# A grouped 3x7 convolution on TensorE: from tiles of 64x64 alone to dense 64x64 tiles plus 32x32 tiles for the single taps

## The chip, the cores and the metric

The kernel runs on one core of a Trainium2 chip (trn2). The metric is the device time of one execution in microseconds (us), the median of the runs. All data and all arithmetic are float32. TensorE is called PE here, its weight loads PEld, VectorE DVE, ScalarE ACT, GpSimd POOL and the engine that issues the DMAs SP, as the profile does.

## The reference

For each of 8 images x of 128 channels and 64x64 pixels:

```
t1  = p1_w * x                        # p1_w: one value for each channel and row
t2  = x + t1
t7  = p7_w @ relu(x)                  # 128x128 over the channels
t12 = mean over the 21 taps of (x - shifted t7)     # five distinct shifts in w
t11 = t1 (128 x 4096) times unfold3x7(x)^T          # 128 x (128*21)
t10 = grouped product of t2 with p10_w              # (128*21) x 4096
out = maximum(t11 @ t10 * scale, t12)
```

The kernel does not build t10 and t11. It first contracts p10_w with the unfolded x for each group of 32 channels, which is a convolution of 3 rows by 7 columns with 32 channels in and 32 out, in 4 groups (y). Then A = y times t1 transposed, a 128x128 matrix for each image, and the output's first operand is A times t2.

## The kernel before, in words

**Units and planes.** There are 32 units (u), one for each image n and group g = u % 4. The three taps in the row direction are done by a minimal-filtering scheme: pairs of image rows and four linear combinations (planes V_0, V_2, V_1, V_3 of `v_planes`, made by DVE from the loaded `xw`), with four planes of weights (`u_planes`, three loaded, then combined by three additions in `weights`). Products with planes 1 and 2 give the sum and difference from which `seeds` makes the starting values of the two banks of the unit, and products with planes 0 and 3 are accumulated on top.

**The seven column taps.** The 64 columns are 16 blocks of 4 phases. The 128 partitions of a plane are 4 phases by 32 channels. A matmul takes 64 partitions (two phases) and gives 64 outputs (a pair of phases by 32 channels) from one block shift, over 512 columns (16 blocks by 32 row pairs). `tiles` does two such matmuls for one shift i and one half of the partitions; together two calls fill the four 64x64 tiles of the array. A unit has four products of planes 1 and 2 (`one_two`, first or second, i of 0 and 1) and four of planes 0 and 3 (`zero_three`). Each of these eight calls issues four matmuls, one in each quarter of the array. The weight tiles hold zeros where a tap falls outside of the seven. In this text such a set of four 64x64 matmuls of 512 columns is called a step. Each float32 matmul shows in the profile as two MATMUL and two LDWEIGHTS records.

**A slot.** The program of PE is written out by hand. In the steady part, `slot(u, ...)` issues the eight convolution steps of planes 1 and 2 of unit u and of planes 0 and 3 of unit u-1, and between them two output items, each with two steps (`outputs_first`, `outputs_second`). An item is one half (512 pixels by 128 channels) of the product p7 with the box sums of relu(x), and another half of the product A times t2. That makes 12 steps. One slot in four has also `y_times_t1`, 32 products of 128 columns, and it is called the y slot here. Slots 0 to 5 and the part after unit 31 are written out apart.

**Dependences inside a slot.** `pq_half`, `m_half` and `item_half` are semaphores by which PE waits for its own earlier matmuls, since the second half of the rows adds to the same place in PSUM. When planes 1 and 2 of u are done (`pq_done`), ACT copies one bank (`copy_two`), DVE computes two seeds (`seeds`), and PE may start planes 0 and 3 of u in the next slot. When those are done (`m_done`), DVE transposes y (`turn_y`), and a new unit may use the banks (three sets) and the planes (three buffers).

**Other work.** DVE also makes the planes of a coming unit (`planes_low`, `planes_high`), the box sums (three operations on 1,024 pixels: `box_pairs`, `box_fours`, `box_last`) and the final maximum (`max_half`, L538). ACT does relu, t2 as eight small activations (`t2_half`, L314), the start values of the p7 banks (`seed_x`) and the copy of p7's result (`base_half`). POOL computes t1 (L219) and the weights of groups 2 and 3. All DMAs are issued by SP in one fixed order, with `load_group` for `xw`. Every order of work is written by hand; there is no planner.

## Time and profile before

| | before |
|---|---|
| median of 3 runs | 413.93 us (413.47 to 414.99) |
| the profiled execution | 411.89 us |
| its span in the profile | 409.9 us |
| PE busy | 398.8 us (97%) |
| DVE busy | 333.6 us (81%) |
| ACT busy | 249.4 us (61%) |
| POOL busy | 90.0 us (22%) |
| DMA | 72.40 MB, mean 177 GB/s |

The span is what the profile shows between the first and the last instruction; the profiled execution took about 2 us more than its span, and the median of the runs is another 2 us above it. A busy PE in this table is PE with at least one matmul running, not PE at its peak, since four tiles of the array can work at once.

### The profile page before, as it was taken

What the parts mean: (1) busy time and instruction counts of PE and PEld (TensorE: products, weight loads), DVE (VectorE), ACT (ScalarE), POOL (GpSimd) and SP (SyncE); (2) the same over time, 40 slices, a digit from 0 to 9 for tenths busy, and PEclk for the clock granted to TensorE, in tenths of its full rate; (3) what the DMA queues carried; (4) which work ended last, traced back from release to release, by engine and by line L of the source; (5) the groups of instructions that cost most, each with busy time, mean ns of one, the idle gap of its engine ahead of it and who ended that gap; (6) DMA issues with size and microseconds to landing.
All of it is one profiled execution on the core that took longest, in us unless ns stands there. A gap on an engine that the chain in (4) does not pass through costs nothing.

```text
span 409.9 us, 12373 instructions
## 1 busy us (share of the span) xinstructions
PE 398.8 (97%) x5126; PEld 250.5 (61%) x5126; DVE 333.6 (81%) x401; ACT 249.4 (61%) x714; POOL 90.0 (22%) x75
## 2 busy tenths in 40 slices
PE   7999999999999999999999999999999999999995
PEld 2333655668655586666888886444766668443663
DVE  6999968899788887888888887888868888786904
ACT  1336728777377755777277771777727775477970
POOL 0582200232023300332003320033202330033300
PEclk9999999999999999999999999999999999999999
DMA  8973263644665447663475635645455542632105
GB/s 295 406 304 109 86 238 116 210 162 158 206 197 176 151 140 221 191 224 104 169 241 201 203 117 187 232 164 164 163 209 187 169 157 80 216 128 95 54 28 206
DMA packets 24104, 72.40 MB, mean 177 GB/s; under 512 B 2800, under 2 KB 3056, under 8 KB 24048
## 3 DMA queue, kind: packets, MB, share of 16 engines
q1 hardware_dynamic: 24048, 71.61, 51.4%
q8 instruction: 41, 0.67, 0.7%
q14 instruction: 15, 0.12, 0.1%
HBM read 54.82 MB, written 16.78 MB: 175 GB/s over the span
## 4 chain that ended last, share of the span: by engine, by line
PE 84%; issue 6%; POOL 3%; DVE 3%; ACT 2%; DMA 2%; DVEq 0%; SPq 0%; ACTq 0%; POOLq 0%
PE ps_y L654 44%; PE ps_y L666 16%; PE ps_p L666 12%; PE ps_t L666 12%; POOL t1T L219 3%; DMA xw<-x_conv 2%; ACT t L314 1%; DVE v_planes L463 0%; DVE v_planes L440 0%; DVE yT L495 0%; DVE v_planes L449 0%; ACT base L259 0%; DVE base L538 0%; ACT relu_pad L272 0%; DVEq L43 0%
## 5 line engine op out<-in xcount | busy, mean ns | idle before, releaser
L654 PE MATMUL ps_y<-v_planes,u_planes 64*64 64x512 f32 x2048 | 257.0, 590 | 0.4
L654 PEld LDWEIGHTS ps_y<-v_planes,u_planes 64*64 64x64 f32 x2048 | 126.1, 133 | 93.6 <-issue 54.7
L219 POOL TENSOR_TENSOR t1T<-t1T,p1T_sb 128x512 f32<-128x512 f32 x64 | 84.1, 1340 | 281.4 <-DVE box L513 152.2
L314 ACT ACTIVATE t<-xn,p_plus 128x64 f32<-128x64 f32 x512 | 128.1, 335 | 0.0
L666 PE MATMUL ps_p<-box,p_fifth 64*64 64x512 f32 x464 | 123.4, 590 | 1.6 <-ACT ps_p L259 1.0
L666 PE MATMUL ps_t<-t,aT 64*64 64x512 f32 x448 | 118.4, 590 | 0.0
L259 ACT ACTIVATE base<-ps_p 128x512 f32<-128x512 f32 x58 | 34.6, 596 | 85.4 <-PE ps_p L666 85.4
L666 PEld LDWEIGHTS ps_y<-t1T,yT 64*64 64x64 f32 x2048 | 58.0, 133 | 8.4 <-DVE yT L495 5.0
L666 PE MATMUL ps_y<-t1T,yT 64*64 64x128 f32 x2048 | 60.7, 270 | 2.0 <-issue 1.2
L666 PEld LDWEIGHTS ps_p<-box,p_fifth 64*64 64x64 f32 x464 | 38.3, 133 | 22.7 <-issue 13.8
L482 DVE SCALAR_TENSOR_TENSOR ps_y<-ps_y,q_sb 128x512 f32<-128x512 f32 x32 | 22.3, 698 | 33.8 <-ACT q_sb L259 33.7
L538 DVE TENSOR_TENSOR base<-ps_t,base 128x512 f32<-128x512 f32 x56 | 38.4, 686 | 12.3 <-PE ps_t L666 11.8
L666 PEld LDWEIGHTS ps_t<-t,aT 64*64 64x64 f32 x448 | 37.2, 133 | 18.0 <-issue 4.9
L505 DVE TENSOR_TENSOR pair_sum<-relu_pad 128x1120 f32<-128x1120 f32 x32 | 42.5, 1328 | 0.0
L495 DVE STREAM_TRANSPOSE yT<-ps_y 128x512 f32<-128x512 f32 x64 | 41.7, 690 | 0.0
L463 DVE TENSOR_TENSOR v_planes<-xw 128x1152 f32<-128x1152 f32 x30 | 41.4, 1381 | 0.0
L522 DVE TENSOR_TENSOR box<-box,relu_pad 128x1024 f32<-128x1024 f32 x32 | 39.1, 1223 | 0.9
L513 DVE TENSOR_TENSOR box<-pair_sum 128x1024 f32<-128x1024 f32 x32 | 39.1, 1223 | 0.8
L259 ACT ACTIVATE ps_p<-xn 128x512 f32<-128x512 f32 x58 | 34.9, 602 | 6.7 <-ACT base L259 0.4
L272 ACT ACTIVATE relu_pad<-xn 128x1024 f32<-128x1024 f32 x32 | 33.7, 1053 | 1.8 <-DVE box L522 1.8
L259 ACT ACTIVATE q_sb<-ps_y 128x512 f32<-128x512 f32 x32 | 18.6, 583 | 24.7 <-PE ps_y L654 24.7
L471 DVE TENSOR_TENSOR v_planes<-xw 128x576 f32<-128x576 f32 x30 | 24.0, 801 | 0.0
(42 smaller groups left out, 119.2 us busy)
## 6 DMA issues: line engine op xcount, KB each, us to landing
xw<-x_conv SPq DMA_DIRECT2D x32, 594.0 KB, 5.4
xn<-x_nat SPq DMA_DIRECT2D x32, 512.0 KB, 4.1
t1T<-x_pix SPq DMA_DIRECT2D x32, 512.0 KB, 6.1
out<-base SPq DMA_DIRECT2D x64, 256.0 KB, 2.5
u_planes<-w_tiles SPq DMA_DIRECT2D x4, 384.0 KB, 7.1
p1T_sb<-p1T SPq DMA_DIRECT2D x1, 128.0 KB, 7.5
p_sb<-p7T SPq DMA_DIRECT2D x1, 64.0 KB, 7.3
p_sb<-p SPq DMA_DIRECT2D x1, 32.0 KB, 7.8
```

What stands on the lines that cost most here:

```text
L219: nc.gpsimd.tensor_tensor(part, part, p1T_sb[:, e, :].unsqueeze(1).broadcast_to([P, 4, C]), ALU.mult).then_inc(t1_ready, 1)
L259: return nc.scalar.activation(dst, src, ACT.Copy, scale=scale)
L272: nc.scalar.activation(relu_pad[:, i % 2, :, LO:LO + W], xn[:, f, :].rearrange("p (a b) -> p a b", b=W), ACT.Relu).then_inc(relu_ready, 1)
L314: last = nc.scalar.activation(t2[:, h, W * r:W * (r + 1)], xn[:, f, at:at + W], ACT.Copy, scale=p1_plus[:, 8 * h + r:8 * h + r + 1])
L463: nc.vector.tensor_tensor(v_planes[:, b, V_0:V_2 + 1], xw[:, b, :, :, 0:PAIRS], second, ALU.subtract).then_inc(v_ready, 1)
L495: nc.vector.transpose(yT[:, e, :, CG * g:CG * (g + 1)], ps_y[u % SETS][e][:].rearrange("p (j r) -> p j r", r=PAIRS)).then_inc(y_turned, 1)
L505: nc.vector.tensor_tensor(pair_sum[:], r[:, :, 0:PS_W], r[:, :, 3:3 + PS_W], ALU.add).then_inc(box_steps, 1)
L513: nc.vector.tensor_tensor(box[:, f, :].rearrange("p (a b) -> p a b", b=W), pair_sum[:, :, 0:W], pair_sum[:, :, 6:6 + W], ALU.add).then_inc ...
L522: nc.vector.tensor_tensor(dst, dst, relu_pad[:, i % 2, :, 12:12 + W], ALU.add).then_inc(box_steps, 1)
L538: nc.vector.tensor_tensor(base[:, h, :], t13_bank(n, h)[:], base[:, h, :], ALU.max).then_inc(out_ready, 1)
L654: last = nc.tensor.matmul(dst[TILE * pair:TILE * pair + TILE, :], u_planes[rows, u % GROUPS, weights, TILE * k:TILE * k + TILE], v_planes[ ...
L666: last = nc.tensor.matmul(dst[cols, 0:data.shape[-1]], weights[rows, cols], data[rows, :], start=start, stop=False, skip_group_check=True)
```

## The change

The seven taps of an output phase are split in another way. For an output pair of phases there are three products of 64 partitions by 64 outputs whose weight tile is full (dense), and what is left are single taps: one 32x32 product for each of the four input phases in each plane. So a plane needs three steps' share of 64x64 tiles and four 32x32 tiles. The three dense calls replace four, and the single taps of four planes (planes 1 and 2 of u, planes 0 and 3 of u-1) are put at the end of the slot as sixteen 32x32 matmuls of 512 columns in sixteen different places of the array (`single_taps`). A semaphore `dense_done` makes PE wait for the dense matmuls before them.

So that the sixteen tiles fall on sixteen places, the phases of x lie on the partitions in different orders: FRONT for planes 0 and 2, BACK for planes 1 and 3, and both differ by the parity of the unit (`PHASES_OF`). x is therefore loaded twice for each unit, with 19 blocks where there were 18: twice 642,048 bytes where there were 608,256. The weights of a group come in both orders: 688,128 bytes where there were 393,216.

`pq_done` of u and `m_done` of u-1 now both come at the end of slot u. In consequence the orders of ACT and DVE are changed: at the start of a slot ACT has `copy_two`, and DVE has `turn_y` and then `seeds`; relu and t2 and the box sums move. In the beginning, the weights are loaded ahead of the x of their group and slots 0 to 3 are written as slots; at the end `turn_y` of the last unit stands before a box sum, and the orders around the last A are changed.

```
-U_0, U_2, U_3, U_1 = range(4)
+FRONT, BACK = range(2)
+U_0, U_2, U_1, U_3 = (FRONT, 0), (FRONT, 1), (BACK, 1), (BACK, 2)
+PHASES_OF = {(0, FRONT): (1, 2, 3, 4), (0, BACK): (3, 4, 1, 2), (1, FRONT): (2, 1, 4, 3), (1, BACK): (4, 3, 2, 1)}
+DENSE = {True: ((0, 1), (0, 2), (1, 2)), False: ((1, 1), (1, 2), (0, 1))}
+SINGLE = {4: (0, 0), 3: (1, 2), 2: (2, 1), 1: (3, 3)}
...
-                sp.dma_start(xw[:, u % 3], x_conv[u // GROUPS, u % GROUPS]).then_inc(xw_loaded[u % 3], 16)
+                for order in range(2):
+                    sp.dma_start(xw[:, u % 3, order], x_conv[u // GROUPS, u % GROUPS, order]).then_inc(
+                        xw_loaded[u % 3][order], 16)
...
+            def dense(u, k, planes, start=False):
+                for half in range(2):
+                    for dst, weights, data in planes:
+                        pair, at = DENSE[low_phases(ORDER_OF[data], half)][k]
+                        last = nc.tensor.matmul(
+                            dst[TILE * pair:TILE * pair + TILE, :], weights_of(rows_of(half), u, weights, TILE * k, TILE),
+                            data_of(rows_of(half), u, data, at), start=start, stop=False, skip_group_check=True)
+                return last
+            def singles(u, planes):
+                for dst, weights, data in planes:
+                    for quarter, phase in enumerate(PHASES_OF[u % 2, ORDER_OF[data]]):
+                        rows = slice(SMALL_TILE * quarter, SMALL_TILE * quarter + SMALL_TILE)
+                        to, at = SINGLE[phase]
+                        last = nc.tensor.matmul(
+                            dst[SMALL_TILE * to:SMALL_TILE * to + SMALL_TILE, :],
+                            weights_of(rows, u, weights, 3 * TILE, SMALL_TILE),
+                            data_of(rows, u, data, at), start=False, stop=False, skip_group_check=True)
+                return last
+            def single_taps(u):
+                pe.wait_ge(dense_done, u + 1)
+                if u < UNITS:
+                    singles(u, planes_12(u)).then_inc(pq_done, 1)
+                if u > 0:
+                    singles(u - 1, planes_03(u - 1)).then_inc(m_done, 1)
...
             def slot(u, p_a, t_a, p_b, t_b, turned=None):
+                one_two(u, 0)
                 outputs_first(p_a, t_a, item_a)
-                one_two(u, True, 0)
+                one_two(u, 1)
                 outputs_second(p_a, t_a, item_a)
                 if turned is not None:
                     y_times_t1(turned)
-                one_two(u, True, 1)
-                zero_three(u - 1, True, 0)
-                zero_three(u - 1, True, 1)
+                one_two(u, 2)
+                zero_three(u - 1, 0)
+                zero_three(u - 1, 1)
                 outputs_first(p_b, t_b, item_b)
-                one_two(u, False, 0)
+                zero_three(u - 1, 2)
                 outputs_second(p_b, t_b, item_b)
-                one_two(u, False, 1)
-                zero_three(u - 1, False, 0)
-                zero_three(u - 1, False, 1)
+                single_taps(u)
```

## Rows read from the trace of the kernel before

**Rows 1.** The page: its first line, then part 1, busy time by engine.
```profile
span 409.9 us, 12373 instructions
...
PE 398.8 (97%) x5126; PEld 250.5 (61%) x5126; DVE 333.6 (81%) x401; ACT 249.4 (61%) x714; POOL 90.0 (22%) x75
```

**Rows 2.** The page, part 5: costliest groups, with busy time, mean ns and idle before.
```profile
L654 PE MATMUL ps_y<-v_planes,u_planes 64*64 64x512 f32 x2048 | 257.0, 590 | 0.4
...
L666 PE MATMUL ps_y<-t1T,yT 64*64 64x128 f32 x2048 | 60.7, 270 | 2.0 <-issue 1.2
```

**Rows 3.** Windows by stage: slots 0 to 3, slots 4 and 5, slots 6 to 31, the rest.
```profile
0.00:33.20 33.20, 30.70 (x234) 10.02 (x238) 29.79 (x36) 9.60 (x20) 13.94 (x15) 1.00 0.81 310
33.20:62.30 29.10, 28.27 (x446) 15.92 (x439) 24.17 (x28) 15.19 (x41) 5.02 (x4) 1.00 0.45 152
62.30:376.40 314.10, 311.79 (x4039) 207.45 (x4039) 262.69 (x316) 204.78 (x590) 67.44 (x54) 1.00 0.53 174
376.40:409.90 33.50, 28.00 (x428) 17.09 (x420) 16.94 (x23) 19.87 (x67) 3.59 (x2) 1.00 0.24 88
```

**Rows 4.** Windows of two plain slots and one y slot: PE, PEld, DVE, ACT, POOL.
```profile
269.50:279.80 10.30, 10.30 (x103) 4.97 (x99) 8.85 (x13) 7.72 (x23) 3.87 (x4) 1.00 0.58 188
...
290.10:308.20 18.10, 17.71 (x359) 13.52 (x355) 14.18 (x18) 8.02 (x24) 0.00 (x0) 1.00 0.56 196
```

**Rows 5.** PEld in order of time at the first steps: start, us, idle before.
```profile
8.52 0.14 PEld L654 LDWEIGHTS ps_y<-v_planes,u_planes 64*64 64x64 f32 x4 [0.29 <-issue]
9.65 0.21 PEld L654 LDWEIGHTS ps_y<-v_planes,u_planes 64*64 64x64 f32 x8 [0.98 <-PE ps_y L654]
10.13 0.15 PEld L654 LDWEIGHTS ps_y<-v_planes,u_planes 64*64 64x64 f32 x4 [0.28 <-issue]
```

**Rows 6.** PE in order of time where the tile size changes.
```profile
6.60 1.06 PE L811 MATMUL ps_p<-relu_pad 128*128 128x512 f32 x1
7.59 1.96 PE L654 MATMUL ps_y<-v_planes,u_planes 64*64 64x512 f32 x16
```

**Rows 7.** DVE in order of time, one plain slot.
```profile
281.01 1.32 DVE L463 TENSOR_TENSOR v_planes<-xw 128x1152 f32<-128x1152 f32 x1
282.25 0.68 DVE L538 TENSOR_TENSOR base<-ps_t,base 128x512 f32<-128x512 f32 x1
...
288.74 0.70 DVE L482 SCALAR_TENSOR_TENSOR ps_y<-ps_y,q_sb 128x512 f32<-128x512 f32 x1 [1.30 <-ACT q_sb L259]
289.48 0.70 DVE L485 SCALAR_TENSOR_TENSOR ps_y<-ps_y,q_sb 128x512 f32<-128x512 f32 x1
290.08 1.30 DVE L495 STREAM_TRANSPOSE yT<-ps_y 128x512 f32<-128x512 f32 x2
```

**Rows 8.** ACT in order of time, part of a slot.
```profile
276.51 0.60 ACT L259 ACTIVATE base<-ps_p 128x512 f32<-128x512 f32 x1 [1.90 <-PE ps_p L666]
277.22 0.60 ACT L259 ACTIVATE ps_p<-xn 128x512 f32<-128x512 f32 x1
277.76 0.58 ACT L259 ACTIVATE q_sb<-ps_y 128x512 f32<-128x512 f32 x1
278.23 2.01 ACT L314 ACTIVATE t<-xn,p_plus 128x64 f32<-128x64 f32 x8
```

**Rows 9.** Windows of the beginning; the last two columns are DMA share and GB/s.
```profile
2.50:5.00 2.50, 2.50 (x4) 0.95 (x4) 1.14 (x2) 0.00 (x0) 0.00 (x0) 1.00 1.01 358
...
20.00:25.00 5.00, 5.00 (x54) 1.70 (x47) 5.00 (x4) 0.63 (x2) 5.00 (x4) 1.00 1.02 409
```

**Rows 10.** DVE in order of time at the start: the first planes and weights.
```profile
4.75 0.76 DVE L436 TENSOR_TENSOR v_planes<-xw 128x576 f32<-128x576 f32 x1 [1.36 <-DMA xw<-x_conv]
...
7.00 0.42 DVE L429 TENSOR_TENSOR u_planes<-u_sum,u_planes 128x256 f32<-128x256 f32 x1
```

**Rows 11.** PE and ACT in order of time near the end.
```profile
386.35 3.72 PE L666 MATMUL ps_y<-t1T,yT 64*64 64x128 f32 x128 [0.41 <-DVE yT L495]
...
397.38 0.27 ACT L259 ACTIVATE a_part<-ps_y 128x128 f32<-128x128 f32 x1
```

More of the change, by code:

```diff
@@ L96, in conv_seq_kernel @@
         small_loaded = sem("small_loaded")
-        xw_loaded = [sem(f"xw_loaded{b}") for b in range(3)]
+        xw_loaded = [[sem(f"xw_loaded{b}{order}") for order in range(2)] for b in range(3)]
         xn_loaded = [sem(f"xn_loaded{f}") for f in range(4)]
@@ new lines, in _ @@
+            t2_half(1, 2)
+            base_half(1, 3)
+            seed_x(1, 4)
+            copy_two(8)
+            relu(2, 0)
+            t2_half(1, 3)
+            base_half(1, 4)
+            seed_x(1, 5)
+            first_part_of_a(1)
+            relu(2, 1)
+            t2_half(1, 4)
+            base_half(1, 5)
+            seed_x(1, 6)
+            t2_half(1, 5)
+            for n in range(2, N_IMG):
+                u = GROUPS * n
+                if n > 2:
+                    copy_two(u - 1)
@@ L566, in _ @@
             planes_high(4)
+            turn_y(2)
             seeds(3)
-            turn_y(2)
             box_sums(0, 1)
+            planes_low(5)
+            planes_high(5)
+            turn_y(3)
+            seeds(4)
+            box_sums(0, 2)
+            planes_low(6)
+            planes_high(6)
+            box_pairs(0, 3)
+            sum_of_a(0)
+            box_fours(0, 3)
+            box_last(0, 3)
+            box_pairs(1, 0)
+            max_half(0, 0)
             for n in range(1, N_IMG):
@@ new lines, in one_two, with zero_three @@
+                last = dense(u, k, planes_12(u), k == 0)
+                if k == 1:
+                    last.then_inc(pq_half, 1)
+                if k == 2 and u == 0:
+                    last.then_inc(dense_done, 1)
+            def zero_three(u, k):
+                if k == 0:
+                    pe.wait_ge(seeded, 2 * u + 2)
+                    pe.wait_ge(v_ready, 3 * u + 3)
+                if k == 2:
+                    pe.wait_ge(m_half, u + 1)
+                last = dense(u, k, planes_03(u))
+                if k == 1:
+                    last.then_inc(m_half, 1)
+                if k == 2:
+                    last.then_inc(dense_done, 1)
```

446 lines of the change are left out of this document (212 added, 234 removed).

## The prediction

> **What bounds the kernel now.** I began with the page's busy times [rows 1]. PE is busy 97% of the span, DVE 81%, ACT 61%. Then I read the costliest groups [rows 2], to see what PE does: 2,048 records of 64x64 by 512 columns for the convolution, 590 ns each, four at a time. The windows by stage [rows 3] split the span into a start of 33.2 us, two irregular slots of 29.1, slots 6 to 31 with 314.1, and an end of 33.5. In the third stage PE is busy 311.8 of 314.1 us. Single slots [rows 4, 7] show what one costs: the transposes of one slot begin 10.30 us before those of the next (289.48 is the seed just ahead of them), and a plain slot has twelve steps, so a step is 10.30 / 12 = 0.858 us, and a half step (one record in each of the four tiles) 0.429 us. All twelve run without a gap. The chain of PE's steps sets the time; DVE has 8.85 of 10.30 us of work in it and ends each slot with a wait of 1.30 us for ACT's copy of q. [...]
>
> **What is removed.** Each unit has six dense steps in place of eight. The sixteen 32x32 products, if they run together, stream 512 columns twice as every step does, so they are one step. A plain slot becomes 11 steps, 9.44 us. In slots 6 to 31, 26 slots, that is 26 x 0.858 = 22.3 us less.
>
> **What the small tiles add.** No record of before has 32x32 tiles, so the price is bounded. Below: nothing, if the array takes tiles of a new size behind running ones. Above, the nearest row is PE waiting for itself [rows 5]: the loads at 8.52 belong to the last half step ahead of a wait and those at 9.65 come after it. Half steps start 0.43 apart, the next would have begun at 8.52 + 2 x 0.43 = 9.38, and the one after the wait takes 10.13 - 9.65 = 0.48 instead of 0.43, as its weights were not loaded ahead. So a full stop with a semaphore costs 0.27 + 0.05 = 0.32 us. Without the semaphore's travel it is the record's tail, 0.590 - 0.429 = 0.16 [rows 2], plus 0.05: 0.21. There are two changes of size in a slot, into the small tiles and out. A load lasts some 0.13 us; four take 0.14 and eight 0.21 [rows 5], so starts follow each other by (0.14 - 0.13) / 3 to (0.21 - 0.13) / 7, 3 to 11 ns. I take 7: sixteen tiles start over 0.10 us. Range for a slot: 0 to 2 x 0.32 + 0.10 = 0.74 us. I take the stop without the semaphore twice, 0.42, plus 0.08 for the staggered start: 0.50 us. The one change of size in this trace [rows 6] speaks neither way: the 128x128 record starts at 6.60 and lasts 1.06, the 64x64 ones start at 7.59, and DVE gave their weights only at 7.00 + 0.42 [rows 10]; so there is at most 0.1 us between weights and matmul.
>
> [...]
>
> `dense_done` costs nothing of its own in a slot: `outputs_second`, one step of 0.858, lies between the last dense step and the wait, more than the 0.27 that a completion takes to come back. `pq_half`, `m_half` and `item_half` each have at least one step between, too. In slots 0 to 3 there is nothing between, and each costs 0.32.
>
> Sum for slots 6 to 31: -22.3 + 26 x 0.50 = -9.3.
>
> **DVE and ACT in a slot.** Both must fit in 9.94 us now. `planes_low` and `planes_high` grow by 1/18: 0.16 us on 1.32 + 0.75 + 0.75. So DVE has 9.0 us in a plain slot. In the y slot it has 14.2 + 0.2 + 1.3 (the `box_pairs` moved in) = 15.7 of about 17.4. It fits, and the wait for q of 1.30 is what paid for it. What has a deadline at the start of a slot: two transposes (1.30), two seeds (0.70 each, 0.73 apart [rows 7]), 0.3 for the completion; done at 3.1 us, and PE wants the seeds after five steps, at 4.3. Next `planes_low` and the first maximum end near 5.1, wanted at 7 steps, 6.0. ACT between slots: p7's copy and the next start value take 0.71 + 0.60 [rows 8]; with the completion (0.27) and the semaphore about 1.7 us, and PE leaves two steps plus the small tiles' extra, 1.7 + 0.5, where it left three steps. Only after the y slot is ACT late: `copy_two` stands behind the eight t2 activations (2.01 us [rows 8]) that stand behind the last start value. Counted from the next slot's start (c being the extra of a slot), start value 0.8 - c, t2 2.7 - c, q 3.3 - c, seeds 4.9 - c: with c = 0.50 that is 4.4 against 4.3, and the maximum behind them at 6.3 against 6.0. I add 0.3 us for six such slots: +1.8. Slots 6 to 31 then come to -7.5.
>
> **DMA.** x is 1.284 MB a unit where it was 0.608: 32 x 0.676 = 21.6 MB more, 72.4 to about 95 MB, with weights. In the steady part that is 174 GB/s [rows 3] plus 0.676 MB x 26 in 306 us, 57 GB/s: 231 of the 409 that the queue reached [rows 9]. It is hidden. POOL's products of t1 keep their gates.
>
> **The start.** There DMA is full from 2.5 to 25 us (share 1.01, 358 and then 409 GB/s [rows 9]). Bytes in order: w0 0.69 MB, x0 1.28, w1 0.69, x1 1.28, w2, x2, small ones, w3, x3. With the first window's 0.90 MB at 358 and then about 400 GB/s, and 1.0 us from the bytes to the landing (x0 of before: 0.61 MB at 3.8, used at 4.75 [rows 10]), x0 is whole at 8.7, its sum plane at 9.5, and PE starts at 9.7 where it started at 7.59 [rows 6]: +2.1. x1 lands at 13.7, just ahead of PE's need at 14.0 (+0.6 for its plane). Then 4 + 7 + 7 + 7 = 25 steps instead of 28, but with eleven uncovered waits at 0.32 (those ahead of the small tiles take the place of the first stop) where before had five, and four slots' second stop. By this account slot 3 ends at 36.2 where it ended at 33.2: +3.0 (between +1.5 and +5, as the DMA rate goes). Slots 4 and 5: two steps fewer (-1.7), +1.0 for small tiles, +0.4 as `early_first(2)` waits for box sums that come later in DVE's order: -0.3.
>
> **The end.** Planes 0 and 3 of unit 31 have three dense steps and half-filled small tiles, so no step is saved; +0.5. Seeds of unit 31 are ready 2.6 us after the slot's end (completion 0.27, q 0.58, seeds 0.73 + 0.70, three semaphores of 0.1) and PE has 2.0 of other work: +0.6 where it was 0.2, so +0.4. The transposes stand ahead of a box sum: y starts 0.56 earlier (of the 0.99 from the last output record to 386.35 [rows 11]). `first_part_of_a`, at 397.38 [rows 11], stays behind t2 and gains 0.2. Together +0.1.
>
> **Sum.** +3.0 - 0.3 - 7.5 + 0.1 = -4.7. The profiled execution's span 409.9 becomes 405.2, its own time 411.9 becomes 407.2. The median of the runs lies 2.0 above that execution, so 413.93 - 4.7 = 409.2, say 409. A change of 0.5% (2 us) is about what the measurement can tell; same means 411.9 to 416.0.
>
> **Rivals.**
> (a) Small tiles cost almost nothing (c about 0.1, the stagger alone). Then 31 x 0.4 = 12.4 us less, but more lateness of ACT after y slots, about 0.4 x 6 = 2.4: 399 us. For it: across different tiles PE already loads and starts independently, since in the y slot the LDWEIGHTS and MATMULs follow without gaps [rows 2]. Against: nothing shows it for another size.
> (b) The other side: the sixteen small products do not run sixteen at a time but eight. Then the stage is two steps, a slot is again 12 steps plus the extra: 31 x 0.858 = 26.6 us more, 436 us. For it: at most four tiles run together anywhere in this trace [rows 2], the float32 stream of four different inputs for each 32 partitions is twice what 64x64 tiles ask, and 64 records must be seen by PE at a time. It decides from a stage longer than 1.2 steps, since 4.7 / 32 = 0.15 us is all that each slot wins.
> [...]
> (c) The handover: both completions now come at the slot's end, and turns, seeds, planes and the first maximum form one chain with 0.9 to 1.2 us of slack, ACT's between slots with about 0.5. If 0.3 us more is lost in each of 26 slots: +8, 417 us. Against: DVE's slot [rows 7] with its present gaps fits.
>
> **How the numbers follow.** My forecast 0.45 (its own range 404 to 414: c from 0.35 to 0.65, start from +1.5 to +5); (a) 0.22; (b) 0.20; (c) 0.13. The range 395 to 425 leaves out (b) and the far end of (a). Faster by over 0.5%: 0.33 of my case, (a), 0.03 of (c): 0.58. Same: 0.09 + 0.04: 0.13. Slower: 0.29.
>
> **What would show it.** 32x32 records whose starts spread over 0.1 us and a gap of some 0.2 us on either side; plain slots 9.9 us apart; PE's first 64x64 at 9.7. A slot of 9.5 would show (a), one of 10.7 or more with small tiles in two or more waves (b), idle PE released by DVE seeds or ACT ps_p (c). My sum is wrong if the two stops are not 0.21 each, or if DMA in the start gets a different rate.

## The result

The changed kernel takes 411.22 us (median of 20 runs, 409.31 to 414.54); the kernel before, timed beside it, 413.46 us (20 runs, 412.13 to 415.10). The ratio is 0.9954, 95% interval 0.9932 to 0.9976: 2.2 us less, where 4.7 were forecast. That lies just within the 0.5% that the prediction called no change. The profiled execution is one of the shorter ones: 409.31 us, its span 407.5.

The page of the changed kernel, its first line, part 1, four of the costliest groups (busy us, mean ns, idle before) and the DMA line, beside [rows 1, 2]:

```profile
span 407.5 us, 13429 instructions
...
PE 386.6 (95%) x5638; PEld 181.5 (45%) x5638; DVE 341.9 (84%) x401; ACT 248.7 (61%) x714; POOL 88.4 (22%) x75
...
DMA packets 28717, 95.29 MB, mean 234 GB/s; under 512 B 3312, under 2 KB 3568, under 8 KB 28656
...
L731 PE MATMUL ps_y<-v_planes,u_planes 64*64 64x512 f32 x1536 | 197.2, 600 | 4.6 <-DVE v_planes L516 3.8
...
L753 PE MATMUL ps_y<-t1T,yT 64*64 64x128 f32 x2048 | 60.2, 270 | 5.4 <-issue 5.3
...
L742 PE MATMUL ps_y<-v_planes,u_planes 32*32 32x512 f32 x1024 | 38.2, 600 | 0.3
```

The dense records fell from 2,048 to 1,536 and 1,024 small ones came. PE is busy 12.2 us less, the span fell by only 2.4: PE is idle more. The products of `y_times_t1` waited 2.0 us in all before [rows 2] and wait 5.4 now. The stages, as in [rows 3] (slots 0 to 3; 4 and 5; 6 to 31; the rest):

```profile
0.00:36.50 36.50, 30.43 (x286) 8.17 (x286) 29.74 (x35) 8.31 (x17) 12.14 (x15) 0.95 0.97 384
36.50:65.80 29.30, 26.54 (x488) 14.36 (x472) 26.49 (x29) 18.03 (x49) 6.12 (x4) 1.00 0.72 267
65.80:374.30 308.50, 303.00 (x4464) 143.85 (x4448) 268.55 (x315) 203.14 (x587) 67.62 (x54) 1.00 0.67 228
374.30:407.50 33.20, 26.60 (x447) 15.11 (x432) 17.16 (x23) 19.26 (x63) 2.51 (x2) 1.00 0.26 97
```

| stage | forecast | measured |
|---|---|---|
| slots 0 to 3 | +3.0 | +3.3 |
| slots 4 and 5 | -0.3 | +0.2 |
| slots 6 to 31 | -7.5 | -5.6 |
| the rest | +0.1 | -0.3 |
| span | -4.7 | -2.4 |

The third stage holds most of the miss: 26 slots, 5.5 us without any PE work (308.50 - 303.00), where 2.3 were idle before [rows 3]. Its plain slots are near the forecast. Here PE around the small tiles, in order of time (start, us, records):

```profile
268.79 0.62 PE L753 MATMUL ps_p<-box,p_fifth 64*64 64x512 f32 x2
269.35 1.14 PE L742 MATMUL ps_y<-v_planes,u_planes 32*32 32x512 f32 x32
270.42 1.10 PE L731 MATMUL ps_y<-v_planes,u_planes 64*64 64x512 f32 x8
```

The 32 records of sixteen small products, which would be 32 x 0.6 us one after the other, take 1.14 us. The last half step ahead starts at 268.79 and leaves room for the next at 269.22 (0.43 later); the small tiles start at 269.35, and the next 64x64 at 270.42, which is 1.07 later where a step is 0.858. So the stage costs 0.13 + 1.07 = 1.20 us, 0.34 above a step; the small rest of the 0.42 by which a slot exceeds eleven steps lies outside of these rows. PE's weight loads in the same place take 0.23 us for all 32 records, in two passes of sixteen, so the sixteen tiles start over 0.1 us. PEld in order of time:

```profile
269.35 0.23 PEld L742 LDWEIGHTS ps_y<-v_planes,u_planes 32*32 32x32 f32 x32 [0.81 <-PE ps_y L731]
```

The transposes of DVE mark the slots. Those of two plain slots begin 9.84 us apart (146.48 - 136.64), forecast 9.94; the two around a y slot 18.05 (164.53 - 146.48):

```profile
136.64 1.31 DVE L555 STREAM_TRANSPOSE yT<-ps_y 128x512 f32<-128x512 f32 x2 [0.57 <-PE ps_y L742]
146.48 1.31 DVE L555 STREAM_TRANSPOSE yT<-ps_y 128x512 f32<-128x512 f32 x2 [0.56 <-PE ps_y L742]
164.53 1.31 DVE L555 STREAM_TRANSPOSE yT<-ps_y 128x512 f32<-128x512 f32 x2
```

Counted by PE's own last records a plain slot is 9.86 us, the slot behind each y slot 10.17 to 10.19 (+0.3, as forecast), and the six y slots are 20.93, 18.04, 17.37, 18.80, 17.37 and 16.92, together 109.4. Before, they were 17.34, 17.47, 18.24, 17.81, 18.10 and 17.66, together 106.6. The longest is the place to look. PE in order of time, the group behind the stall (in brackets the idle time before it), and under it windows of the same stretch (PE, PEld, DVE, ACT, POOL busy; granted clock, DMA share, GB/s):

```profile
109.12 0.97 PE L753 MATMUL ps_y<-t1T,yT 64*64 64x128 f32 x25 [2.73 <-issue]
```

```profile
101.00:106.90 5.90, 5.40 (x192) 5.15 (x184) 5.72 (x7) 0.60 (x1) 0.00 (x0) 1.00 0.94 331
106.90:109.10 2.20, 0.00 (x0) 0.00 (x0) 0.00 (x0) 0.00 (x0) 0.00 (x0) 1.00 0.11 36
```

From 101.0 to 106.9 the DMA engines are 94% busy: SP issued both orders of x for a coming unit at 100.04, the place where the old kernel issued one. When they are done, PE stands still for more than 2 us inside `y_times_t1`, with 26 of its 256 records to go (25 of them in the row above). No engine works, so none released it. "Issue" says only that the trace shows nothing that it waits for. The waits of that line in the changed kernel (total us, times, longest us); the old kernel's totals were 5.4 and 1.2 us:

```profile
PEld ps_y L753 <- issue: 14.3, 24, 3.0
...
PE ps_y L753 <- issue: 5.3, 4, 2.7
```

### The profile page after: what moved, and what is told of

Read it like the earlier page. It is cut to its first block, busy times and chain, and to the rows that moved or that the text cites. A ratio compares the mean times of both kernels' runs of the same rounds, so it can differ in the third digit from the quotient of the medians.

```text
span 407.5 us, 13429 instructions
## 1 busy us (share of the span) xinstructions
PE 386.6 (95%) x5638; PEld 181.5 (45%) x5638; DVE 341.9 (84%) x401; ACT 248.7 (61%) x714; POOL 88.4 (22%) x75
## 4 chain that ended last, share of the span: by engine, by line
PE 83%; DVE 9%; issue 4%; DMA 2%; ACT 1%; DVEq 0%; SPq 0%; ACTq 0%
PE ps_y L731 36%; PE ps_y L753 16%; PE ps_p L753 12%; PE ps_t L753 11%; PE ps_y L742 8%; DVE box L573 2%; DMA xw<-x_conv 2%; DVE pair_sum L565 2%; DVE yT L555 1%; DVE v_planes L510 1%; DVE v_planes L516 1%; DVE ps_y L542 1%; DVE base L598 1%; DVE v_planes L534 1%; DVE box L582 1%
## 5 line engine op out<-in xcount | busy, mean ns | idle before, releaser
L731 PE MATMUL ps_y<-v_planes,u_planes 64*64 64x512 f32 x1536 | 197.2, 600 | 4.6 <-DVE v_planes L516 3.8
L237 POOL TENSOR_TENSOR t1T<-t1T,p1T_sb 128x512 f32<-128x512 f32 x64 | 82.5, 1316 | 277.3 <-DVE box L582 238.7
L753 PE MATMUL ps_p<-box,p_fifth 64*64 64x512 f32 x464 | 120.1, 590 | 2.2 <-DVE box L582 1.7
L753 PE MATMUL ps_t<-t,aT 64*64 64x512 f32 x448 | 116.2, 591 | 0.1
L731 PEld LDWEIGHTS ps_y<-v_planes,u_planes 64*64 64x64 f32 x1536 | 63.5, 133 | 113.7 <-issue 88.1
L753 PEld LDWEIGHTS ps_y<-t1T,yT 64*64 64x64 f32 x2048 | 57.9, 133 | 11.7 <-issue 10.8
L510 DVE TENSOR_TENSOR v_planes<-xw 128x1216 f32<-128x1216 f32 x31 | 48.2, 1555 | 0.2 <-DMA xw<-x_conv 0.2
L753 PEld LDWEIGHTS ps_p<-box,p_fifth 64*64 64x64 f32 x464 | 34.0, 133 | 30.2 <-issue 21.1
L753 PEld LDWEIGHTS ps_t<-t,aT 64*64 64x64 f32 x448 | 32.5, 132 | 27.1 <-issue 12.5
L565 DVE TENSOR_TENSOR pair_sum<-relu_pad 128x1120 f32<-128x1120 f32 x32 | 43.2, 1350 | 0.0
L573 DVE TENSOR_TENSOR box<-pair_sum 128x1024 f32<-128x1024 f32 x32 | 41.1, 1283 | 0.6
L742 PE MATMUL ps_y<-v_planes,u_planes 32*32 32x512 f32 x1024 | 38.2, 600 | 0.3
L274 ACT ACTIVATE q_sb<-ps_y 128x512 f32<-128x512 f32 x32 | 18.6, 581 | 21.8 <-PE ps_y L742 21.8
## 6 DMA issues: line engine op xcount, KB each, us to landing
p1T_sb<-p1T SPq DMA_DIRECT2D x1, 128.0 KB, 12.2
p_sb<-p SPq DMA_DIRECT2D x1, 32.0 KB, 12.2
```

What stands on the lines that cost most here:

```text
L237: nc.gpsimd.tensor_tensor(part, part, p1T_sb[:, e, :].unsqueeze(1).broadcast_to([P, 4, C]), ALU.mult).then_inc(t1_ready, 1)
L274: return nc.scalar.activation(dst, src, ACT.Copy, scale=scale)
L510: nc.vector.tensor_tensor(v_planes[:, b, V_0:V_2 + 1], xw[:, b, FRONT, :, :, 0:PAIRS], second, ALU.subtract).then_inc(ready, 1)
L565: nc.vector.tensor_tensor(pair_sum[:], r[:, :, 0:PS_W], r[:, :, 3:3 + PS_W], ALU.add).then_inc(box_steps, 1)
L573: nc.vector.tensor_tensor(box[:, f, :].rearrange("p (a b) -> p a b", b=W), pair_sum[:, :, 0:W], pair_sum[:, :, 6:6 + W], ALU.add).then_inc ...
L731: last = nc.tensor.matmul(dst[TILE * pair:TILE * pair + TILE, :], weights_of(rows_of(half), u, weights, TILE * k, TILE), data_of(rows_of(h ...
```

## The experiments

Eleven kernels ran on the chip, each timed beside the kernel before. Medians and ratios are against it. The question was where the steady part's time stays, and then what the head and each size change cost.

| run | edit | median us (runs) | ratio (95%) |
|---|---|---|---|
| e1_warm | after + three zero matmuls at the start | 408.41 (6) | 0.9909 (0.9874 to 0.9943) |
| e2_same_size | after, four 64x64 for the sixteen 32x32 | 401.49 (4) | 0.9723 (0.9694 to 0.9751) |
| e3_one_order | after, second order of x not reloaded | 404.85 (6) | 0.9825 (0.9781 to 0.9868) |
| e4_quiet_y | after, one x load issued later | 402.76 (5) | 0.9746 (0.9717 to 0.9774) |
| e5_before_quiet_y | before, the same move | 409.78 (4) | 0.9913 (0.9898 to 0.9928) |
| e6_before_x_twice | before + x loaded again, unread | 425.88 (4) | 1.0298 (1.0281 to 1.0315) |
| e7_quiet_warm_head | e4 + e1 + orders of slot 4 | 401.06 (6) | 0.9699 (0.9685 to 0.9714) |
| e8_and_q_early | e7 + `copy_two` ahead of t2 | 399.60 (4) | 0.9668 (0.9653 to 0.9682) |
| e9_two_stages | after, small tiles in two stages | 436.61 (4) | 1.0581 (1.0544 to 1.0619) |
| e10_after_again | after, unchanged | 411.77 (12) | 0.9953 (0.9927 to 0.9979) |
| e11_split_y | after, `y_times_t1` in two halves | 411.52 (12) | 0.9971 (0.9952 to 0.999) |

### e1_warm: PE's clock in the head

In the changed kernel PE waits 2.77 us for the first planes, and its clock is granted at half (0.51 from 8.4 to 11.9 us) in the first steps. PE in order of time and the windows of that stretch:

```profile
8.77 4.66 PE L731 MATMUL ps_y<-v_planes,u_planes 64*64 64x512 f32 x24 [2.77 <-DVE v_planes L516]
```

```profile
8.40:11.90 3.50, 3.13 (x16) 0.80 (x16) 2.27 (x5) 0.00 (x0) 0.00 (x0) 0.51 1.00 415
```

```
+            for _ in range(3):
+                nc.tensor.matmul(ps_p7[:], zeros[:, 0:P], zeros[:, 0:HALF], start=True, stop=True)
             for bank_set in (ps_p7[:, 0:HALF // 2], ps_t13, ps_p7):
```

> The changed kernel with three more matmuls of zeros (128x128 by 512 columns) at PE's beginning, so that PE is busy until about 8.4 us instead of 5.9. In the profile of the changed kernel PE is idle from 6 to 8.8 us, its granted clock falls to half at 8.5 us and stays there until 11.9, and the first four half steps take 0.83 to 0.93 us instead of 0.43. Theory (the clock costs time in the start, and in some executions more of it): the first half steps take 0.43, the granted clock of the whole is 1.000, the profile's stage of slots 0 to 3 is shorter by 0.5 to 1.7 us, and the median falls by 1 to 2.5 us, to 409 to 410, with less spread. Rival (x of units 1 and 2 sets the start, landing by landing): the first half steps are faster, but slot 3 ends as before at 36.5 and the median stays within 0.5 us of the changed kernel's.

The gap is filled and the clock is full. PE's first dense record and the same window in this kernel:

```profile
10.00 3.12 PE L731 MATMUL ps_y<-v_planes,u_planes 64*64 64x512 f32 x24
```

```profile
8.40:11.90 3.50, 3.50 (x20) 0.89 (x18) 2.38 (x5) 0.00 (x0) 0.00 (x0) 1.00 1.01 417
```

Yet slots 0 to 3 end at 36.2 instead of 36.5. The steps started 1.2 us later and ran at twice the speed (the first three half steps 0.43 to 0.48 us each where they were 0.85 to 0.91), and then PE waited for x either way: of 4.66 us for the 24 records against 3.12 little is kept, while DMA is full (share 1.01). The median fell by 2.8 us, but the intervals of the two ratios overlap; the ratios differ by 0.0045, or 1.9 us. The trace shows 0.3 us in the head, and that too is within what heads differ by without this edit: in e9, whose program is the changed kernel's up to slot 5, PE waited 2.11 us and then took the same 24 records in 3.12 us, and slots 0 to 3 ended 1.1 us sooner than in the changed kernel. PE in order of time in e9:

```profile
8.91 3.12 PE L732 MATMUL ps_y<-v_planes,u_planes 64*64 64x512 f32 x24 [2.11 <-DVE v_planes L517]
```

So what the edit is worth is not shown; the rival, that the landings of x set the head, fits better than the theory.

### e2_same_size: what do two changes of tile size cost?

```
-                    singles(u, planes_12(u)).then_inc(pq_done, 1)
+                    large(u, planes_12(u), 0).then_inc(pq_done, 1)
...
-                    singles(u - 1, planes_03(u - 1)).then_inc(m_done, 1)
+                    large(u - 1, planes_03(u - 1), 1).then_inc(m_done, 1)
```

`large` issues two 64x64 products of 512 columns for each pair of planes, so the stage is an ordinary step of four. The single taps are left out, a dense tile is repeated in their place.

> The changed kernel with the sixteen 32x32 products at the end of a slot replaced by four 64x64 products of 512 columns, at the same place behind the same wait (the single taps are left out, and a repeated dense tile is added in their place). Theory (what the small stage costs above one step is the change of tile size, twice in a slot): plain slots of 11 x 0.858 = 9.44 us instead of 9.85, the whole 32 x 0.41 = 13 us shorter, unless DVE or ACT become the limit. Rival (the extra is the wait dense_done and its semaphore): plain slots stay at 9.85. Second rival (DVE and ACT have no room left): slots between 9.44 and 9.85 with PE waiting for DVE or ACT.

DVE in order of time, the transposes of the same two plain slots and of the y slot behind them:

```profile
131.63 1.31 DVE L555 STREAM_TRANSPOSE yT<-ps_y 128x512 f32<-128x512 f32 x2 [0.35 <-PE ps_y L751]
141.19 1.31 DVE L555 STREAM_TRANSPOSE yT<-ps_y 128x512 f32<-128x512 f32 x2 [0.35 <-PE ps_y L751]
158.17 1.30 DVE L555 STREAM_TRANSPOSE yT<-ps_y 128x512 f32<-128x512 f32 x2
```

A plain slot is 9.56 us (141.19 - 131.63), by PE's records too. Eleven steps are 9.44. So of the 0.42 that a slot of the changed kernel costs above eleven steps, 0.30 (9.86 - 9.56) goes with the tile size and 0.12 stays with the same shapes. The wait for `dense_done` is still there and is the likely cause of the 0.12, though no run took it out. I had taken 0.50: 0.42 for two full stops and 0.08 for the stagger. Two changes of size cost less than two full stops, about 0.15 each. They do not cost nothing either: 0.30 us for two, with the stagger of 0.1 in it. Of the 9.7 us by which the median fell (13 were expected) part lies in the y slots: this program has fewer records, and its stalls stand at other places.

### e3_one_order and e4_quiet_y: is it DMA that holds up `y_times_t1`?

The prediction called DMA hidden. The rival explanation of the long y slots is that DVE or ACT are late there, since both carry more between slots. Two edits take traffic out of the stretch. e3 loads the second order of x for the first three units only; the BACK planes of later units are made of stale data (18.6 MB less):

```
-                for order in range(2):
+                for order in range(2 if u < 3 else 1):
...
-            dve.wait_ge(xw_loaded[b][BACK], 16 * (u // 3 + 1))
+            dve.wait_ge(xw_loaded[b][BACK], 16)
```

e4 loads every byte, but issues one of the four x loads of each image at another place in SP's order, behind the load of t1, which waits for the end of `y_times_t1`:

```
                 load_natural(n, 1)
-                load_group(u + 4)
                 store(n - 2, 7)
                 load_pixels(n)
+                load_group(u + 4)
```

> The changed kernel with x in the second order loaded for the first three units only (later units compute planes 1 and 3 from stale data): 18.6 MB less DMA in all, 0.642 MB for each unit from the fourth. Theory (PE's instruction fetches are late in y_times_t1 because data DMAs are in their way; idle time of PE inside y_times_t1 put down to issue is 7.0 us over the six y slots of slots 6 to 31, where it was 2.6 before the change): the idle time goes back to 2.6 or less, the y slots fall from 18.2 to about 17.4 us in the mean, and the median falls by 4 to 5 us. Rival (the stalls come from where the ends of the fetched pieces fall within the program, whatever the DMA): no change beyond 1 us, stalls of 0.4 to 3 us at the same y slots.

> The changed kernel with one load moved in SP's order: the two loads of x for unit u+4 are issued behind the pixel loads, which wait for the end of y_times_t1, so that 1.28 MB less flows while y_times_t1 runs. Bytes in all are the same. Theory (data DMAs delay instruction fetches in the y slot): idle time inside y_times_t1 falls from 7.0 us in six y slots to under 2, the median falls by 4 to 5 us. Rival (place of the pieces in the program): the idle time stays. Second rival (total traffic): it stays too, and it falls only with fewer bytes.

The waits by line of e3:

```profile
PEld ps_y L753 <- issue: 9.7, 21, 2.5
...
PE ps_y L753 <- issue: 1.4, 2, 1.1
```

The waits by line of e4, and its windows: the third stage, and PE in the y slot of the third image (compare 149.70 of the changed kernel, below it):

```profile
PEld ps_y L753 <- issue: 8.8, 21, 2.5
...
PE ps_y L753 <- issue: 0.5, 2, 0.3
```

```profile
65.90:368.20 302.30, 301.75 (x4464) 138.17 (x4448) 268.58 (x315) 203.28 (x587) 67.72 (x54) 1.00 0.67 236
147.70:154.70 7.00, 7.00 (x256) 6.80 (x252) 6.07 (x7) 1.24 (x3) 0.00 (x0) 1.00 0.11 40
```

```profile
149.70:157.90 8.20, 7.31 (x261) 7.15 (x257) 6.43 (x7) 1.47 (x4) 0.00 (x0) 1.00 0.47 186
```

e4's DMA share in the stage is the changed kernel's, 0.67, and its rate no lower (236 GB/s against 228, the same bytes in less time). DVE's and ACT's work is the same to 0.2 us. Only the place of a load differs, and PE's idle time in the stage falls from 5.5 to 0.55 us and the stage from 308.5 to 302.3. Four of the six y slots are 16.84, the length without any wait, one is 17.36, and the first is 18.38. The median is 8.5 us lower, where 4 to 5 were expected, and this one edit makes the changed kernel faster than the old one by 2.5%. With e3 a y slot is 16.84 to 16.88 except for two (19.28 and 17.62), and its median is 6.4 us lower. So lateness of DVE or ACT is refuted, and that DMA traffic at the time of `y_times_t1` holds PE up is shown, by amount (e3) and by time alone (e4).

### e5_before_quiet_y: did the old kernel have it too?

The same move in the old kernel.

> The kernel before the change, with the load of x for unit u+4 (0.61 MB) issued behind the pixel loads, which wait for the end of y_times_t1; nothing else. Theory (data DMAs delay PE's instruction fetches in y_times_t1, before the change too): the idle time inside y_times_t1, 2.1 us over the six y slots of slots 6 to 31 in the profile, goes to under 0.5, and the median falls by 1.5 to 3 us, so that the gain of the tiles alone is about 411 against 403 us. Rival (the change made these stalls, the old kernel's are of another kind): no change beyond 0.5 us.

Its third stage is 313.4 us long (314.1 before), of which PE is busy 311.12: the window in one row.

```profile
61.30:374.70 313.40, 311.12 (x4038) 228.72 (x4039) 262.25 (x316) 204.82 (x590) 67.54 (x54) 1.00 0.52 175
```

The wait did not fall below 0.5 us as I had expected: by this trace it is 1.3 us where it was 1.2. The six y slots are 106.0 us together where they were 106.6; four are within 0.04 of 17.29, the length without a stall, but the first, 17.34 before, is now 18.88, with a stall of 0.89 in it. So in its profile the old kernel gained next to nothing in the y slots, and the expectation on the wait was wrong. The median fell by 3.5 us; the two profiled spans differ by 1.7 (409.9 to 408.2), the old kernel's profiled execution being 2 us below its median and this one's 0.3 above. What the pair e5 and e4 gives is what the tiles are worth with the load moved in both, which leaves about as much of the stalls in one as in the other (2.3 and 2.1 us in the six y slots): 409.8 to 402.8, 7.0 us. By their traces: the third stage 313.4 to 302.3, -11.1; up to its beginning 61.3 to 65.9, +4.6; the end -0.3; together -6.8.

### e6_before_x_twice: the old kernel with the new kernel's traffic

```
                 sp.dma_start(xw[:, u % 3], x_conv[u // GROUPS, u % GROUPS]).then_inc(xw_loaded[u % 3], 16)
+                if u >= 3:
+                    wait(sp, spare_loaded, 16 * (u - 3))
+                    sp.dma_start(spare[:], x_conv[u // GROUPS, u % GROUPS]).then_inc(spare_loaded, 16)
```

Nothing reads `spare`; 17.6 MB more are moved and no engine has more work.

> The kernel before the change, with x of each unit from the fourth loaded a second time into a spare buffer that nobody reads (0.61 MB a unit more, 17.6 MB in all), right behind the first load. Only the traffic of the change is added, none of its tiles. Theory (traffic in y_times_t1 delays the instruction fetches): idle time inside y_times_t1 rises from 2.1 to 4 to 7 us over six y slots, and the median rises by 2 to 5 us, while plain slots stay at 10.30. Rival (place of the fetched pieces in the program): no change in either, since the program of PE is the same.

It cost 12.6 us, not 2 to 5. The waits of that line (longest last), and two windows around a y slot with the granted clock ahead of the last two columns:

```profile
PEld ps_y L671 <- issue: 14.0, 13, 3.1
PE ps_y L671 <- issue: 9.5, 6, 2.9
```

```profile
254.00:256.80 2.80, 0.94 (x32) 0.70 (x28) 1.28 (x2) 0.00 (x0) 0.00 (x0) 1.00 0.30 108
256.80:260.50 3.70, 3.70 (x56) 2.73 (x52) 1.32 (x2) 0.28 (x1) 0.00 (x0) 0.54 0.18 34
```

The wait grew from 1.2 to 9.5 us, and the six y slots from 106.6 to 119.8 us. After a stretch in which PE worked a third of the time the clock is granted at about half for 3.7 us, so a stall costs more than itself: 3.7 us at 0.54 do the work of 2.0. In the next y slot, from within a wait of 2.9 us on, it was at half for 6.8 us:

```profile
308.10:314.90 6.80, 5.72 (x74) 4.74 (x78) 1.59 (x3) 0.28 (x1) 0.00 (x0) 0.51 0.17 32
```

The traffic alone, with no new tiles, does the damage.

### e10_after_again: why does the changed kernel spread over 5 us?

> The changed kernel itself once more, for a second profile and its times on this chip. In its 20 timed executions so far the span is 407.5 to 410.6 us where the mean granted clock is 0.996 and 411.7 to 412.7 where it is 0.988 or 0.989. Theory (stalls inside y_times_t1 differ from execution to execution, and in the long ones the clock falls as well): the y slots differ between the two profiles by up to some us while plain slots stay at 9.86 to 10.19; if this execution is a long one, half clock stands at a y slot. Rival (the spread is made in the start, where PE waits for x): the end of slot 3 differs and the y slots do not.

Its profiled execution had a span of 410.2 us. The head is the same to 0.2 us; the y slots are 24.17, 18.15, 17.10, 18.36, 17.25 and 16.84. PE in order of time in the longest, and windows of the stall and of what follows:

```profile
110.91 1.53 PE L753 MATMUL ps_y<-t1T,yT 64*64 64x128 f32 x25 [4.26 <-issue]
```

```profile
107.70:111.20 3.50, 0.29 (x10) 0.29 (x14) 0.00 (x0) 0.00 (x0) 0.00 (x0) 1.00 0.22 78
111.20:114.60 3.40, 3.40 (x38) 2.44 (x34) 1.52 (x2) 1.90 (x6) 0.00 (x0) 0.50 0.27 51
```

It is the stall of the changed kernel's profile in the same place, 4.26 instead of 2.73 us, and this time the clock fell to half behind it (0.50 for 3.4 us, 1.7 us of work lost). The first y slot is 3.2 us longer and the span 2.7; the other five are within 0.5 of the first profile's. So the stalls come back at the same places, and their length differs. What lies between these two executions comes from them, and e4, which has few of them, has its five runs within 1.4 us.

### e11_split_y: shorter bursts of short products

If PE needs its instructions faster in `y_times_t1` (its products are 128 columns wide, a quarter of the others), two halves with two steps between them should stall less with the same DMAs.

```
                 outputs_first(p_a, t_a, item_a)
+                if turned is not None:
+                    y_times_t1(turned, 0, BLOCKS)
                 one_two(u, 1)
                 outputs_second(p_a, t_a, item_a)
                 if turned is not None:
-                    y_times_t1(turned)
+                    y_times_t1(turned, BLOCKS, 2 * BLOCKS)
                 one_two(u, 2)
```

> The changed kernel with y_times_t1 in two halves of 16 products each in `slot`: the first behind outputs_first, the second behind one dense step and outputs_second as the whole was. The DMAs, their bytes and their order are the changed kernel's. In y_times_t1 PE takes a record every 14 ns or so, in the steps with 512 columns one every 54 ns, so the two steps between the halves give a late instruction fetch 1.7 us more. Theory (what is late is PE's next piece of program, because data DMAs are ahead of it): idle time inside y_times_t1 over the six y slots falls from 6.4 or 7.2 us in the two profiles to under 3, and the median falls by 3 us or more, less what PE waits in the first half for the transposes (up to 0.4 us each). Rival (the traffic itself stops PE's reads or writes while it flows): the idle time stays at 5 to 8 us, since the traffic flows at the same time as before.

The waits by line of this kernel:

```profile
PEld ps_y L753 <- issue: 11.7, 24, 2.4
...
PEld ps_y L753 <- DVE yT L555: 5.3, 8, 1.8
PE ps_y L753 <- issue: 2.4, 4, 0.8
```

PE's "issue" wait halved (5.3 to 2.4), but the first half now waits for DVE's transpose, and the slots behind the y slots are 10.2 to 10.8. The six y slots are together 109.0 where they were 109.4, and the median did not fall by the 3 us expected: 411.52 against 411.77 for e10. The stall near the end of the first `y_times_t1` is still there with the same 25 records in the group behind it, but it is 0.61 where it was 2.73 and 4.26. PE in order of time:

```profile
110.09 0.98 PE L753 MATMUL ps_y<-t1T,yT 64*64 64x128 f32 x25 [0.61 <-issue]
```

The wait can be shared out, but it does not go away. By the idle time the theory is borne out, by the median it is not; as a test of the cause the run alone is inconclusive.

### e9_two_stages: a second pair of size changes

The singles of planes 1 and 2 come right behind `zero_three(u - 1, 1)`, those of planes 0 and 3 at the slot's end; each stage fills half of the array.

```
                 zero_three(u - 1, 1)
+                pe.wait_ge(pq_dense, u - 5)
+                singles(u, planes_12(u)).then_inc(pq_done, 1)
                 outputs_first(p_b, t_b, item_b)
                 zero_three(u - 1, 2)
                 outputs_second(p_b, t_b, item_b)
-                single_taps(u)
+                pe.wait_ge(dense_done, u + 1)
+                singles(u - 1, planes_03(u - 1)).then_inc(m_done, 1)
```

> The changed kernel with the small stage split in slots 6 to 31: the eight 32x32 products of planes 1 and 2 directly behind the second dense step of planes 0 and 3, the other eight at the end of the slot, each behind a wait that one or two steps of other work cover. So each slot has four changes of tile size instead of two, and two half-filled small stages instead of a full one. Theory (two changes cost 0.30 us together, as the run with one tile size says: 9.86 - 9.56; a half-filled stage lasts one step): plain slots of 9.86 + 0.86 + 0.30 = 11.0 us, of which DVE and ACT have 9.0 or less to do. Rival (the extra of 0.42 comes once a slot, from the wait dense_done and the loads behind it): 10.7. Second rival (eight small tiles stream faster than sixteen): under 10.7.

The transposes of a plain slot (DVE in order of time), and a half-filled stage (PE in order of time):

```profile
298.13 1.31 DVE L556 STREAM_TRANSPOSE yT<-ps_y 128x512 f32<-128x512 f32 x2 [0.40 <-PE ps_y L743]
...
309.07 1.32 DVE L556 STREAM_TRANSPOSE yT<-ps_y 128x512 f32<-128x512 f32 x2 [0.40 <-PE ps_y L743]
```

```profile
304.13 1.09 PE L743 MATMUL ps_y<-v_planes,u_planes 32*32 32x512 f32 x16
305.14 0.65 PE L754 MATMUL ps_p<-box,p_fifth 64*64 64x512 f32 x2
```

A slot is 10.94 us, 1.08 more than 9.86 and close to the 11.0 of the theory: one step, 0.858, and 0.22 for the second pair of changes. Eight small products take nearly as long as sixteen (1.01 us from 304.13 to 305.14, where sixteen took 1.07 to 1.12), so putting all sixteen in one stage is what makes the change pay; two stages cost 25.4 us over the one.

### e7_quiet_warm_head and e8_and_q_early: what else is to be had

In slots 4 and 5 the changed kernel's PE waits once for the planes of unit 4 and once for box sums. e7 is e4 and e1 together, with DVE's planes of unit 4 ahead of the last two box operations, and PE's `early_first(2)` behind the dense steps:

```
             seeds(2)
-            box_fours(0, 0)
-            box_last(0, 0)
             planes_low(4)
             planes_high(4)
+            box_fours(0, 0)
+            box_last(0, 0)
...
             zero_three(3, 1)
-            early_first(2)
             zero_three(3, 2)
+            early_first(2)
             early_second(2)
```

> The changed kernel with the quiet y_times_t1 (loads of x for unit u+4 behind the pixel loads), the three more matmuls of zeros at the start, and two moves in slots 3 and 4: DVE makes the planes of unit 4 ahead of the last two box operations of the first item (PE waited 1.2 us for these planes at 36 to 37.7 us), and PE issues the last dense step of unit 3 ahead of the output item of slot 4 (PE waited 1.8 us for box sums at 43 to 45.7). Against the quiet kernel's 402.8: theory (both waits are on the path, since DVE has room behind them): slot 5 ends at 63 to 64 us in the profile instead of 65.9, the median is 400 to 401.5. Rival (what DVE does later is then late, the stall moves to unit 5 or to A of image 0): slot 5 still ends at 65 to 66.

401.06 us against 402.76 for e4; the two intervals nearly touch (0.9685 to 0.9714 and 0.9717 to 0.9774), and the profiled execution is the longest of the six (403.24). In it slots 0 to 3 end at 35.2, but the clock was at half from 39.8 to 43.2 us, behind a wait of 2.15 us, and slot 5 ended no earlier than in e4; 63 to 64 was expected. How much each of the three edits gives is not shown: e9's head was as short to 0.2 us without them. e8 adds the answer to the 0.3 us behind each y slot: ACT copies q ahead of the last eight t2 activations.

```
                     seed_x(n - 1, 6)
-                    t2_half(n - 1, 5)

                 copy_two(u + 1)
+                t2_half(n - 1, 5)
```

> As the kernel with quiet y_times_t1, more zeros and the moves in slots 3 and 4, and ACT's copy of q for the y slot's unit ahead of the eight t2 activations instead of behind them (2.0 us earlier). Theory (the slot behind each y slot takes 10.18 us instead of 9.86, as q and with it the seeds come late): those slots fall to 9.86, six times 0.32, 1.9 us less than the kernel without it. Rival (the late maximum, or the p7 start value behind it, sets these slots): they stay at 10.1 to 10.2, since t2 then delays p7's copy.

The third stage in one window:

```profile
64.80:364.60 299.80, 299.69 (x4464) 138.67 (x4448) 265.81 (x315) 203.19 (x587) 67.73 (x54) 1.00 0.68 238
```

PE is idle for 0.11 us of 299.80. The slots behind the y slots are 9.94 to 9.96 where they were 10.18 (9.86 was expected), so most of the lateness was ACT's order. At 399.60 us it is the fastest complete kernel here, 3.3% below the old one and 2.8% below the change as made.

## Why the prediction came out as it did

**The step that failed: "It is hidden", of DMA.** The prediction compared an average of 231 GB/s in the steady part with the 409 that the queue had reached. The average was right (228 measured). But the traffic comes in bursts, at 331 GB/s and 94% in the window from 101.0 to 106.9 us, and the place of one of them is `y_times_t1`, where PE has more instructions in a microsecond than anywhere else (508 records of PE and PEld in 7.00 us in e4, 73 in a us; 16 in a step of 0.858, 19 in a us). The six y slots, without a stall, would take 16.84 each, 101.0 in all; they took 109.4, an excess of 8.4, where before it was 106.6 - 6 x 17.29 = 2.9. That is +5.5 us which no term of the sum held. (PE's idle time in the stage grew by 3.2 only, from 2.3 to 5.5: the rest is time in which its products trickle, with one short record at work, and the page counts that as busy. The wait of PEld for the same products has it: 14.3 us in the changed kernel, 8.8 in e4, which has few stalls.) e4 takes it away with the same bytes, e3 with fewer, and e6 puts it into the old kernel.

**What cancelled part of it.** Two terms were sized too dear. The small stage costs 0.42 a slot, not 0.50, inside the forecast's own bounds: 26 x 0.08 = -2.1. Its parts came out otherwise: 0.30 for the two changes with the stagger, where 0.50 was taken, and 0.12 that stays with one tile size, where `dense_done` was put at nothing. That each change of size is a full stop of 0.21 was the author's estimate, and no run shows it; what e2 shows is 0.30 for the two with the stagger. And slot 6, which held a wait of 1.4 us before (11.74 us long by PE's records), is now 9.86; the forecast had kept that wait. The third stage then comes out as 26 x -0.436 (10.30 to 9.86) = -11.3, +1.9 behind the y slots, -1.4 and +5.5: -5.3 against -5.6 measured. Beside this stage's 1.9 us, the span misses the forecast by 0.8 in the stages ahead of it and is 0.4 better at the end, 2.3 in all.

**What held.** Eleven steps in place of twelve, and sixteen products at once in float32: rival (b) is refuted in every small stage of slots 6 to 31, which takes 1.07 to 1.12 us and not 2 x 0.858. The sixteen starts lie some 7 ns apart, 0.10 us in all, as taken from rows in the prediction. Rival (a), nothing for the change of size, is refuted by e2. Rival (c), the handover's chains: +0.3 came behind the y slots only, as forecast, and was ACT's order of work (e8). The start was +3.3 against +3.0, though not by the steps given: PE started at 8.77 and not 9.7, and then ran at half clock. In e1 the head changed by only 0.3 us when both changed, and e9's head differs by 1.1 with the same program, so the nearness is in part luck. The end was 0.4 us better.

**What the stalls are, and what stays open.** "Issue" means that the profile shows nothing that PE waits for, so what it waits for has to be inferred. The stored traces bear on it in three ways. First, in the stall at 106.9 us the only transfer of note is one of 16 KB in the queue that the page calls instruction. It ends at 107.81, and PE goes on 1.31 us later, at 109.12. DMA in the window from 106.1 to 109.2:

```profile
q8 instruction: 1, 0.02, 1.9%
```

In e10 it ends at 109.66, and PE goes on at 110.91. The same holds everywhere: the thirteen profiles have 44 such stalls inside `y_times_t1` (over 0.3 us between the starts of two records, put down to "issue"), and each ends 1.2 to 1.6 us after the end of a 16 KB transfer of that queue. Second, a stall keeps its place in the count of records and not in time or in the work: the one of the first y slot stands behind 2,712 records of PE and PEld together in the changed kernel and in e1, e3, e4, e7, e9, e10 and e11. In e1 and e7 three more matmuls of zeros put 12 more records ahead, six of them PE's, and the stall has moved to six PE records earlier in `y_times_t1`, with 32 left instead of 26. PE in order of time in e1 and in e9:

```profile
108.28 1.10 PE L753 MATMUL ps_y<-t1T,yT 64*64 64x128 f32 x32 [2.35 <-issue]
```

```profile
110.82 0.97 PE L754 MATMUL ps_y<-t1T,yT 64*64 64x128 f32 x25 [3.04 <-issue]
```

Third, the traffic does not hold PE up while it flows: PE took 192 records in the 5.9 us with DMA 94% busy, and stood still behind them. The author's reading of the three: PE's next piece of program comes late behind x's packets; the count of instructions sets where, and the traffic sets how long. This is inferred from times and places in the traces: the profile does not say for which engine a transfer of that queue is, and no run moved such a transfer by itself.

## What to carry to other kernels

A mean transfer rate says nothing about whether a transfer is hidden: find the stretch in which an engine takes the most instructions in a microsecond (here the products of 64x64 by 128 columns, 270 ns each, four at a time), and keep bursts of bulk loads out of it. One load moved down in the queue was worth 8.5 us here, more than the new tiling itself (7.0). A stall without a semaphore that keeps its place in the count of instructions from kernel to kernel (here behind 2,712 records in eight of them) is a reason to look at the queue that the page calls instruction. When a change adds traffic, lay the added bytes over the timeline by slot, not over the span; and before judging the change, take its traffic into the old kernel and its order out of the new one, since the two effects had opposite signs and nearly cancelled.

## What the runs showed of the hardware

Unread loads of 17.6 MB cost 12.6 us (413.3 to 425.9, e6) in a kernel whose DMA share in the third stage was 0.53 without them. PE stood still inside `y_times_t1` where the profile shows nothing that it waits for, in the changed kernel's two profiles (its own and e10) behind the same counts of records (2,712, 3,967 and 6,733 in both), and went on 1.2 to 1.6 us after the end of a 16 KB transfer of the instruction queue (44 stalls in thirteen profiles). PE's clock was granted at half after it had stood nearly still (2.77 us without work in the head of the changed kernel, 2.15 in e7, 4.3 in e10, about a third busy for 2.8 us in e6) and stayed there for some 3.4 us, in e6 once for 6.8; a single wait of 2.73 us in the changed kernel's profile and one of 2.11 in e9's head left it at full. A change between 64x64 and 32x32 tiles and back cost 0.30 us with the stagger of sixteen starts (e2), a second pair in the slot 0.22 (e9). Eight 32x32 products of 512 columns took 1.01 us to the next matmul (e9), sixteen 1.07 to 1.12.
